# Dividing the softmax weights before they are turned, with the values as the stationary operand

## The reference, cut to what matters

```
q, k, v = split(shift_tokens(x) @ Wqkv)              # 16 heads of 64
q, k = l2norm(q) * qs, l2norm(k) * ks                # then rotated by cos and sin tables
sim  = einsum('bhwie,bhwje->bhwij', q, k2) * 8       # 32 queries against 64 keys in each window
attn = softmax(where(mask, -max, sim))
out  = einsum('bhwij,bhwje->bhwie', attn, v2)
x    = concat_heads(out) @ Wo + x
x    = ffn(shift_tokens(x)) + x                      # layer norm, up, gelu gate, down
```

## Time and profile before

| | us |
|---|---|
| median of 3 runs | 2470.04 (2466.25 to 2470.73) |
| the profiled execution | 2455.97 |
| its span, first to last instruction | 2454.2 |
| TensorE busy (share of the span) | 2001.6 (82%) |
| TensorE weight loads | 1355.8 (55%) |
| GpSimd | 1665.2 (68%) |
| VectorE | 1635.7 (67%) |
| ScalarE | 1246.8 (51%) |

### The profile page before, as it was taken

How to read it: one execution, slowest core, us unless ns; L and a number is a source line. 1 busy time by engine, 2 the same in 40 slices (tenths; PEclk the granted TensorE clock), 3 DMA queues, 4 the chain that set the end, 5 groups by cost and what they waited for, 6 DMA issues and landing times.

```text
span 2454.2 us, 76245 instructions
## 1 busy us (share of the span) xinstructions
PE 2001.6 (82%) x33704; PEld 1355.8 (55%) x33800; DVE 1635.7 (67%) x1873; ACT 1246.8 (51%) x1330; POOL 1665.2 (68%) x992
## 2 busy tenths in 40 slices
PE   3678898588888888888888888888888888888885
PEld 1234443365656665656565666666565656565664
DVE  5556661576777677777776677667767776777664
ACT  1145455454555555555555555555555455545541
POOL 1000000998889887897888888878788889797851
PEclk7589999799999999999999899999999999999998
DMA  2311100122222222232222222222222223222221
GB/s 86 105 46 34 46 22 19 36 68 57 58 74 61 59 58 72 57 80 58 57 71 58 69 65 54 58 68 74 55 61 55 73 55 85 55 57 53 60 59 51
DMA packets 133726, 146.72 MB, mean 60 GB/s; under 512 B 60946, under 2 KB 76304, under 8 KB 132628
## 3 DMA queue, kind: packets, MB, share of 16 engines
q1 hardware_dynamic: 133396, 141.84, 23.0%
HBM read 30.83 MB, written 5.44 MB: 15 GB/s over the span
## 4 chain that ended last, share of the span: by engine, by line
PE 61%; DVE 13%; issue 11%; ACT 7%; POOL 4%; SPq 2%; DMA 1%; DVEq 0%; POOLq 0%; ACTq 0%
PE banks L472 10%; PE banks L481 7%; PE banks L554 7%; PE banks L571 5%; PE banks L537 5%; PE banks L498 4%; PE banks L519 4%; DVE arena L743 3%; PE banks L545 3%; PE banks L409 3%; PE banks L511 3%; ACT arena L988 3%; PE banks L580 3%; DVE arena L646 2%; PE banks L392 2%
## 5 line engine op out<-in xcount | busy, mean ns | idle before, releaser
L1095 POOL TENSOR_TENSOR arena<-arena,tab_sl 128x512 f32<-128x512 f32 x384 | 459.4, 1229 | 153.9 <-ACT arena L963 153.3
L1077 POOL TENSOR_TENSOR rn<-ss,minus_half 128x32 f32<-128x32 f32 x96 | 524.0, 5459 | 8.0
L1103 POOL TENSOR_TENSOR arena<-arena 128x1024 f32<-128x1024 f32 x192 | 450.4, 2369 | 68.9 <-DVE arena L790 68.9
L472 PE MATMUL banks<-w_qkv,arena 128*128 128x512 f32 x768 | 349.2, 598 | 9.4 <-ACT arena L955 9.4
L481 PE MATMUL banks<-ident,arena 128*128 128x128 f32 x1536 | 253.5, 332 | 109.2 <-DVE arena L790 75.9
L743 DVE TENSOR_TENSOR arena<-arena,rn 128x1024 f32<-128x1024 f32 x192 | 286.8, 1534 | 82.7 <-POOL rn L1077 82.6
L973 ACT COPY arena<-banks 128x1024 f32<-128x1024 f32 x96 | 97.9, 1020 | 444.1 <-PE banks L481 444.1
L537 PE MATMUL banks<-arena 64*32 64x64 f32 x12288 | 178.4, 227 | 141.5 <-issue 141.5
L481 PEld LDWEIGHTS banks<-ident,arena 128*128 128x128 f32 x1536 | 223.4, 174 | 124.1 <-DVE arena L790 80.7
L963 ACT COPY arena<-banks 128x1024 f32<-128x1024 f32 x192 | 194.2, 1012 | 182.9 <-PE banks L472 182.9
L646 DVE TENSOR_REDUCE arena<-banks 128x1 f32<-128x1024 f32 (+7 forms) x176 | 175.1, 1027 | 126.8 <-PE banks L373 126.5
(11 more groups left out here) (107 smaller groups left out, 3334.4 us busy)
## 6 DMA issues: line engine op xcount, KB each, us to landing
arena<-arena SPq DMA_DIRECT2D x1512, 64.0 KB, 2.0
w_qkv<-Wqkv SPq DMA_DIRECT2D x6, 1024.0 KB, 5.4
arena<-parts_dram SPq DMA_DIRECT2D x96, 48.0 KB
arena<-parts_dram SPq DMA_DIRECT2D x32, 144.0 KB
parts_dram<-arena SPq DMA_DIRECT2D x4, 768.0 KB, 3.3
w_o<-Wo SPq DMA_DIRECT2D x6, 512.0 KB
w_qkv<-Wqkv SPq DMA_DIRECT2D x6, 512.0 KB, 4.4
arena<-X SPq DMA_DIRECT2D x24, 128.0 KB
```

The lines of the kernel that those rows point to most:

```text
L472: last = e.matmul(ps[:, BANK * c:BANK * (c + 1)], xsT[b][:, P * t:P * (t + 1)], w_qkv[:, at:at + BANK], start=True, stop=True)
L1077: e.tensor_tensor(rn[n % 2][:, :], ss[n % 2][:, :], minus_half[:, :], ALU.pow).then_inc(S["rn"], 1)
L1095: e.tensor_tensor(qk_sw[:, m, :].rearrange("p (h d) -> p h d", d=HEAD_DIM)[:, :, d:d + HALF], raw[:, m, :].rearrange("p (h d) -> p h d", d ...
L1103: e.tensor_tensor(to, to, qk_sw[:, m, :], ALU.add).then_inc(S["rs"], 1)
```

## The change

The division by the softmax sums moves from the output of the value product to the exponentials themselves: `normalise` now works in SBUF on 128x1024 exponentials in place, right behind `sums` of the same tile, and signals `p_norm`, for which `weights_turn` waits. In `gather` the operands change places. The values are stationary, 64 rows and 64 columns, and 32 columns of turned weights move, so the output of a head stands on 64 partitions (its dimensions) with the queries along the columns. That is the layout that `output` needs; `outputs_turn` goes, ScalarE's `outputs` copies the product itself, and `output` reads the chunks in another order. `output` of tile s-4 moves on TensorE ahead of `gather`, ScalarE's `outputs` ahead of `turn`. The table of PSUM pairs follows, with nine products in a plain step where ten were.

```diff
@@ the table of PSUM pairs @@
                 place(("sc", s - 2), 4, "sub", s - 2 + 1)
+            if 0 <= s - 4 < n_tiles:
+                place(("wo", s - 4), 4, "x_attn", s - 4 + 1)
             if 0 <= s - 3 < n_tiles:
-                place(("pv", s - 3), 4, "o_norm", 2 * (s - 3) + 2)
+                place(("pv", s - 3), 4, "ot", s - 3 + 1)
...
                 place(("pT", s - 2), 4, "pt", s - 2 + 1)
-            if 0 <= s - 3 < n_tiles:
-                place(("oT", s - 3), 4, "ot", s - 3 + 1)
...
-            if 0 <= s - 4 < n_tiles:
-                place(("wo", s - 4), 4, "x_attn", s - 4 + 1)
@@ TensorE @@
             def weights_turn(n):
                 ps = pair("pT", n)
-                w.wait_ge(S["ex"], n + 1)
+                w.wait_ge(S["p_norm"], n + 1)
...
-                for c in range(CHUNKS):
-                    half, i = divmod(c, CHUNKS // 2)
-                    at = P * i + HEAD_DIM * half
+                for c in range(CHUNKS // 2):
                     for hp in range(2):
                         r = slice(64 * hp, 64 * hp + 64)
                         for i in range(WPT):
                             q = slice(WINDOW * i, WINDOW * (i + 1))
-                            last = e.matmul(ps[q, BANK * hp + HEAD_DIM * c:BANK * hp + HEAD_DIM * (c + 1)],
-                                            PT[n % 2][r, c, q], Vw[n % 3][r, i, at:at + HEAD_DIM], start=True, stop=True)
+                            at = BANK * hp + P * c + WINDOW * i
+                            for half in range(2):
+                                d = HEAD_DIM * half
+                                last = e.matmul(ps[d:d + HEAD_DIM, at:at + WINDOW], Vw[n % 3][r, i, P * c + d:P * c + d + HEAD_DIM],
+                                                PT[n % 2][r, CHUNKS // 2 * half + c, q], start=True, stop=True)
                 last.then_inc(S["pv"], 1)
-
-            def outputs_turn(n):
-                ps = pair("oT", n)
-                w.wait_ge(S["o_norm"], 2 * n + 2)
-                for c in range(CHUNKS):
-                    last = e.transpose(ps[:, P * c:P * (c + 1)], O[n % 2][:, P * c:P * (c + 1)], ident)
-                last.then_inc(S["oT"], 1)
...
                 if 0 <= s - 2 < n_tiles:
                     score(s - 2)
+                if 0 <= s - 4 < n_tiles:
+                    output(s - 4)
                 if 0 <= s - 3 < n_tiles:
                     gather(s - 3)
...
-                if 0 <= s - 3 < n_tiles:
-                    outputs_turn(s - 3)
...
-                if 0 <= s - 4 < n_tiles:
-                    output(s - 4)
@@ VectorE @@
             def normalise(n):
...
-                w.wait_ge(S["pv"], n + 1)
                 w.wait_ge(S["recip"], n + 1)
-                w.wait_ge(S["oT"], max(0, n - 1))
-                for hp in range(2):
-                    e.tensor_tensor(to[:, hp], ps[:, hp], rs[:, hp].unsqueeze(3).to_broadcast([P, 2, CHUNKS // 2, HEAD_DIM]),
-                                    ALU.mult).then_inc(S["o_norm"], 1)
+                e.tensor_tensor(PB[n % 2], PB[n % 2], rs_o[n % 2][:, :].unsqueeze(2).to_broadcast([P, HEADS, 2 * WINDOW]), ALU.mult
+                                ).then_inc(S["p_norm"], 1)
...
-                if 0 <= s - 3 < n_tiles:
-                    normalise(s - 3)
...
                 if 0 <= s - 2 < n_tiles:
                     sums(s - 2)
+                    normalise(s - 2)
@@ ScalarE @@
             def outputs(n):
-                w.wait_ge(S["oT"], n + 1)
+                w.wait_ge(S["pv"], n + 1)
...
+                if 0 <= s - 3 < n_tiles:
+                    outputs(s - 3)
                 if 0 <= s - 1 < n_tiles:
                     turn(s - 1)
```

More of the change, by code:

```diff
@@ L99 @@
 tab_c tab_s halves_set zero_xs zero_xf xsT xs_ready proj raw sq ss_sum floor rn rc sw rs rot tk tq kt_ready qt_ready kp
-sc mx sub v_proj v_ready vw_first ex sm recip pT pt pv o_norm oT ot wo x_attn
+sc mx sub v_proj v_ready vw_first ex sm recip p_norm pT pt pv ot wo x_attn
 f_stat f_mv f_var f_rstd xf_norm f_nT xft h gel u f_out x_add x_ff final""".split()
@@ L216, in build @@
         Vw = [stack(WPT, INNER // 2) for _ in range(3)]
-        O = [stack(INNER) for _ in range(2)]
         OT = stack(CHUNKS, P)
@@ L553, in output @@
                 for c in range(CHUNKS):
-                    last = e.matmul(ps[:, 0:P], OT[:, c, :], w_o[l % 2][:, c, :], start=c == 0, stop=c == CHUNKS - 1)
+                    last = e.matmul(ps[:, 0:P], OT[:, c % 2 * (CHUNKS // 2) + c // 2, :], w_o[l % 2][:, c, :], start=c == 0, stop=c == CHUNKS - 1)
                 last.then_inc(S["wo"], 1)
@@ L755, in sums @@
                 w.wait_ge(S["ex"], n + 1)
-                w.wait_ge(S["o_norm"], max(0, 2 * (n - 1)))
+                w.wait_ge(S["p_norm"], max(0, n - 1))
                 e.tensor_reduce(sm_t[:, :], PB[n % 2], AX_X, ALU.add).then_inc(S["sm"], 1)
@@ L761, in normalise @@
             def normalise(n):
-                ps = banks[:, pair_of["pv", n], :].rearrange("p (hp f i d) -> p hp f i d", hp=2, f=2, d=HEAD_DIM)
-                rs = rs_o[n % 2][:, :].rearrange("p (f i hp) -> p hp f i", f=2, hp=2)
-                to = O[n % 2].rearrange("p (i hp f d) -> p hp f i d", hp=2, f=2, d=HEAD_DIM)
-                w.wait_ge(S["pv"], n + 1)
                 w.wait_ge(S["recip"], n + 1)
-                w.wait_ge(S["oT"], max(0, n - 1))
-                for hp in range(2):
-                    e.tensor_tensor(to[:, hp], ps[:, hp], rs[:, hp].unsqueeze(3).to_broadcast([P, 2, CHUNKS // 2, HEAD_DIM]),
-                                    ALU.mult).then_inc(S["o_norm"], 1)
+                e.tensor_tensor(PB[n % 2], PB[n % 2], rs_o[n % 2][:, :].unsqueeze(2).to_broadcast([P, HEADS, 2 * WINDOW]), ALU.mult
+                                ).then_inc(S["p_norm"], 1)
             def subtract(n):
@@ L995, in outputs @@
             def outputs(n):
-                w.wait_ge(S["oT"], n + 1)
+                w.wait_ge(S["pv"], n + 1)
                 w.wait_ge(S["wo"], n)
-                e.copy(OT.rearrange("p c q -> p (c q)"), banks[:, pair_of["oT", n], :]).then_inc(S["ot"], 1)
+                e.copy(OT.rearrange("p c q -> p (c q)"), banks[:, pair_of["pv", n], :]).then_inc(S["ot"], 1)
             def ff_gelu(G):
@@ L1021, in scalar_program @@
                     weights(s - 2)
-                if 0 <= s - 3 < n_tiles:
-                    outputs(s - 3)
                 if s % GROUP == GROUP - 1 and s + 1 < n_tiles:
```

## The result

The changed kernel takes 2822.39 us (median of 4 runs, 2816.88 to 2828.02) against 2468.14 beside it: 1.144 times as long, 95% interval 1.1406 to 1.1473. The profiled execution took 2824.9 us, its span is 2823.1. The forecast was 2863 for the median, 41 us too much, and 2849 for the profiled execution, 24 too much. The two forecasts start from different times of the kernel before: the median of three runs (2470.04) and the profiled execution (2455.97).

The account below looks back on a forecast made before the run. TensorE was taken to bound three of four kinds of step, VectorE the fourth (k 2). Terms summed to 16.56 us a round, 393 over 95 steps; added to 2455.97 this gave 2849 profiled, 2863 median; range 2690 to 3080.

Parts of the forecast that it names:

- The wait: Ahead of the v projection: v waits for residual, starting 7.24 us after turn starts, formerly 1.81; TensorE idles 5.3 us.
- its nearer row: VectorE's new division: the sum over the same exponentials, 1.22 us, judged nearer than a scaling of 1.545; 1.25 taken.
- The value products: In gather on TensorE: 128 instructions a tile in the new shape, between 1.5 and 7.2 us; 3.6 taken.
- Two loads at a time, 28 ns an instruction: In gather: 64-column loads of 56 ns each overlap in pairs, giving 3.6 us for 128.
- The clock: On TensorE behind the new idle: the granted clock falls to 1.2 GHz, charged 1.2 us in steps without such idle today.
- up to 1.9 more: In the v projection: upper bound in us on its added time if it runs at the lower clock.
- `output`: On TensorE, moved ahead of gather: same 1.79 us length at another place, no gain in itself.
- The issue wait: Ahead of and within gather: 1.3 to 1.9 us from two bursts in a row, charged at nothing after the move.
- The clock keeps up: Rival on TensorE's new idle: no clock charge, 2770 us; chance 0.24 together with a quick gather.
- Gather is slow: Rival in the value products: 5.4 us gives 3034, all loads in turn at 7.2 us gives 3205; chance 0.2.
- The residual is no hindrance: Rival ahead of v: residual done when turn ends, so v covers the softmax again; 2465 us, no change; chance 0.03.
- that rotation time, 29.0 us: In the k 2 step: rotation ready 29.0 us after the k 1 step's start, said not to hold the step.

Follow-up runs that it names:

- residual_early: The changed kernel with VectorE's residual moved from behind the division to right behind subtract; 2612.42 us, 1.0617 times the kernel before.
- order_alone: The kernel before with output moved ahead of gather on TensorE, residual left last on VectorE; 2671.35 us, 1.0833 times the kernel before.
- one_tile: The changed kernel with gather's loops reordered, half and row pair outermost, so 32 instructions in a row use the same array quarter; 3606.45 us, one run.
- four_tiles: The changed kernel with gather's loops reordered, half and row pair innermost, so four array quarters take turns product by product; 2790.3 us, one run.
- output_ahead: The kernel before with output ahead of gather on TensorE and residual right behind subtract on VectorE; 2378.63 us, 0.9667 times the kernel before.
- keep_busy: The changed kernel with 22 unread bf16 products of 512 columns between turn and the v projection; 2623.97 us, 1.0661 times the kernel before.
- gather_behind_turn: The changed kernel with residual early, value products behind turn on TensorE, ScalarE's outputs behind its exponents; 2447.65 us, 0.9935 times the kernel before.

## Why the prediction was right

**The wait.** The step that carried the forecast held: v's pair, the residual, `turn` to v. 7.24 us was put, 7.07 measured (1410.93 to 1418.00); with k 0 8.52 was put and 8.47 measured. residual_early and order_alone show the cause from both sides. The division took the 1.22 us that its nearer row had.

**The value products: mis-sized.** 3.6 us was put, 2.45 measured (1408.48 to 1410.93). The step that failed is "Two loads at a time, 28 ns an instruction". Its first half, 56 ns for a 64-column load by itself, is near what one_tile shows at full clock, about 53. The overlap was put too small: in this order an instruction takes 19 ns from start to start (2.45 us for 128), nearly three in the time of one, and 17 in four_tiles. Why two quarters in turn give more than a factor of two stays open. Over a round 4.6 us were charged too much.

**The clock: mis-sized the other way.** 1.2 us a step was put. v alone takes 3.46 to 3.58 from start to start instead of 1.81, and with k 2 and k 0 the turned weights 1.7 instead of 0.87; with what follows, 9.1 us a round where 4.8 was charged. The choice of 1.2 rested on the earlier trace rows, where only part of v lay at the low clock. The bound "up to 1.9 more" was the better row to take.

**`output`: put at no gain and no loss.** At its new place it takes 1.98 us from start to start (1406.50 to 1408.48) and not 1.79, 0.8 us a round. output_ahead, with the old layout, has 1.98 as well (1417.61 to 1419.59), so it is the place and not the layout.

The errors nearly cancel, which is luck: the closeness of the total, 24 us on the profiled execution, proves less than it seems. By kind of step: k 1 21.38 (22.1 put), k 2 23.04 (22.4), k 3 26.98 (28.0), k 0 26.63 (25.8). In this round that is 16.3 us more than before, where 16.56 was put. Most of the 24 us comes from letting one round stand for all: over 22 rounds of each trace the mean goes from 82.1 to 97.6 us, 15.5 a round.

**The issue wait** is gone, as charged: 0.5 us in the middle of the run. order_alone and output_ahead confirm that it belongs to the two bursts in a row. That instructions arrive more slowly than the bursts use them is a reading; no run shows it.

**The rivals.** "The clock keeps up" is refuted, and keep_busy gives it a price: 2624, not the 2770 worked out, which had the value products 1.15 us a step too long and a late rotation in the k 2 step that didn't come (20.32 us, 1421.88 to 1442.20). "Gather is slow" fell in this order of the loops; in one_tile's order the value products took 8.31 us, more than its top of 7.2. "The residual is no hindrance" was rightly held unlikely, but its price was wrong in three ways: it took gather at 1.5 us, the clock would have fallen in the 3 us that it left, and the k 2 step could get shorter, because `ff_norm` isn't of fixed length. The forecast took that rotation time, 29.0 us, as a constant. After the change it didn't bind, which hid the error there.

## What to carry to other kernels

When an instruction is moved in a kernel that hands out PSUM in rotation, work out anew who frees the buffer of each product behind it; a wait can land on a product that has no other tie to it, and here that was worth more than the edit itself. Ask of each product what it covers before its start is made later. And where a new idle of TensorE is as long as those here (3.3 to 6.5 us), look whether the clock falls in it, and add the half-clock work to its price only where what follows isn't waiting for something else.

## What the runs showed of the hardware

- In residual_early the granted clock fell in an idle of TensorE of 3.27 us, with full clock before it: 0.58 of full speed in the 3.7 us behind it. The forecast had looked at idles of some 5 us. In order_alone it stayed full through one of 3.79 us. And in one_tile it fell with no idle at all, in the midst of small products at 53 ns each.
- VectorE's 128x128 subtract-and-multiply in SBUF takes 353 ns on average in the changed kernel and 952 in output_ahead, where GpSimd's multiplications run beside it (756 before). The division takes 1.22 us in the changed kernel, beside GpSimd's reciprocal root. In gather_behind_turn it takes 1.22 us beside the root too, and 1.3 to 2.3 where it starts beside the addition. The Trainium skill, "GPSIMD Engine Reference", in the table at its head, row on SBUF interfaces, says that GpSimd shares them with VectorE and that VectorE's instructions in a 2-port mode or with two SBUF inputs contend. The trace agrees for the addition: the division has two such inputs. It shows no cost beside the root, a difference that the row doesn't make; and whether the subtract-and-multiply runs in a 2-port mode no trace shows.
- At full clock, small float32 products with 64x64 loads run at some 17 to 53 ns an instruction by order alone, and in the slowest order at about 98 where the clock is at half. On the load itself the Trainium skill's rule, "TensorE: Matmul & The Clock Gate", section on LDWEIGHTS, makes 53 ns of 64 columns (an estimate from its figure). The trace agrees in one_tile's order at full clock; at half clock it takes nearly twice as long, for which the rule has no term. The 17 and 20 ns are below it, so there the loads for different quarters overlap.
